# Style steps on ScalarE and GpSimd, one block's z on VectorE, and identity sums in transposing mode

## The reference, cut to what matters

```
# layer 0: adapter, per token
h  = gelu(x @ down_W.T + down_b)                 # 128 -> 32
h  = expert_W[dom] @ h + expert_b[dom] + emb[dom]
x1 = layernorm(h @ up_W.T + up_b + x) * ln_gamma + ln_beta
# layer 1, per block
z  = (x1 - mean) * rsqrt(var + 1e-5)             # per token
h  = z * ln_g + ln_b, normalised over the 256 tokens of the block
se = subj_emb[id];  hyp = relu(se @ hyp_w1 + hyp_b1) @ hyp_w2 + hyp_b2
gamma, beta = split(relu(hyp @ sty_w1 + sty_b1) @ sty_w2 + sty_b2)
gamma = softplus(gamma) + 1e-8
h  = h * gamma + beta                            # style of the block
gates = top 2 of softmax(h @ router_w), renormalised
y  = sum over 8 experts of gate * (relu(h @ w1 + b1) @ w2 + b2)   # 128 -> 512 -> 128
out = x1 + y
```

## Time and profile before

| | |
|---|---|
| median of 3 runs | 119.39 us (118.95 to 119.65) |
| profiled execution, device time | 119.94 us |
| its span in the trace | 118.2 us |
| busy PE / PEld / DVE / ACT / POOL | 112.0 / 84.3 / 91.8 / 84.3 / 54.1 us |
| chain that ended last, largest | PE 72%, DVE 14%, ACT 5%, issue 3%, DMA 3% |
| first expert matmul | at 19.66 us |
| last expert matmul | starts at 112.67 us |
| last output transfer issued | at 115.88 us |

### The profile page before, as it was taken

One profiled execution on the slowest core, in us unless ns is written; L12 is line 12 of the kernel. 1 busy time (PEld: TensorE's weight loads), 2 busy tenths in 40 slices (PEclk: granted clock), 3 DMA queues, 4 the chain that ended last, 5 costly groups with the idle time before them and its releaser, 6 DMA issues.

```text
span 118.2 us, 1665 instructions
## 1 busy us (share of the span) xinstructions
PE 112.0 (95%) x519; PEld 84.3 (71%) x519; DVE 91.8 (78%) x228; ACT 84.3 (71%) x153; POOL 54.1 (46%) x75
## 2 busy tenths in 40 slices
PE   6799988999999999999999999999999999999990
PEld 2157534777777888688888888888888888888780
DVE  4486988999899989997685959595867777776772
ACT  2139845698999988697878787878778687878400
POOL 5020889226417000101259999976758941322310
PEclk9999999999999999999999999999999999999999
DMA  4939699994000000326999300000000000000005
GB/s 68 343 97 365 173 374 442 384 412 150 0 0 3 0 6 0 89 100 165 415 446 408 169 0 6 0 0 0 0 0 0 0 0 0 6 0 0 0 0 178
DMA packets 4473, 14.17 MB, mean 120 GB/s; under 512 B 561, under 2 KB 1905, under 8 KB 4209
## 3 DMA queue, kind: packets, MB, share of 16 engines
q1 hardware_dynamic: 3024, 9.67, 21.9%
q0 software_dynamic: 1008, 3.67, 8.8%
q10 hardware_dynamic: 432, 0.73, 2.2%
HBM read 13.52 MB, written 0.56 MB: 119 GB/s over the span
## 4 chain that ended last, share of the span: by engine, by line
PE 72%; DVE 14%; ACT 5%; issue 3%; DMA 3%; POOL 1%; DVEq 0%; ACTq 0%; POOLq 0%
PE bank L594 22%; PE bank L595 22%; PE bank L633 12%; PE bank L613 11%; DMA ids_i<-ids_dram 3%; DVE x L913 2%; ACT hid_high L508 2%; DVE stats L920 1%; ACT bank L511 1%; DVE hid_low L1005 1%; DVE bank L905 1%; POOL z L370 1%; PE bank L750 1%; DVE stats L876 1%; PE bank L583 1%
## 5 line engine op out<-in xcount | busy, mean ns | idle before, releaser
L508 ACT ACTIVATE hid_high<-bank,early_sb 128x512 fp32r<-128x512 f32 x64 | 44.2, 691 | 15.9 <-PE bank L613 15.8
L1005 DVE TENSOR_TENSOR hid_low<-bank,hid_high 128x512 fp32r<-128x512 f32 x51 | 34.8, 687 | 16.7 <-ACT bank L511 16.1
L511 ACT ACTIVATE bank<-bank,early_sb 128x512 f32<-128x512 f32 x51 | 33.6, 658 | 0.0
L308 POOL TENSOR_TENSOR w_low<-w_raw,w_high 128x256 fp32r<-128x256 f32 x32 | 22.7, 734 | 12.3 <-DMA w_high<-w_all_dram 4.4
L633 PE MATMUL bank<-hid_low,w_high 128*128 128x512 f32 x64 | 25.9, 405 | 0.4 <-DVE hid_low L1010 0.2
L594 PE MATMUL bank<-h_high,w_low 128*128 128x512 f32 x64 | 25.5, 398 | 0.3 <-ACT h_high L486 0.3
L594 PE MATMUL bank<-hid_high,w_low 128*128 128x512 f32 x64 | 25.6, 400 | 0.0
L595 PE MATMUL bank<-h_high,w_high 128*128 128x512 f32 x64 | 25.3, 396 | 0.0
L613 PE MATMUL bank<-h_low,w_high 128*128 128x512 f32 x64 | 25.1, 397 | 0.0
L595 PE MATMUL bank<-hid_high,w_high 128*128 128x512 f32 x64 | 25.0, 390 | 0.0
L318 POOL TENSOR_TENSOR y_sum<-y_sum,y_part 128x512 f32<-128x512 f32 x9 | 11.6, 1292 | 17.3 <-DVE y_part L1025 15.1
(11 more groups left out here) (136 smaller groups left out, 99.2 us busy)
## 6 DMA issues: line engine op xcount, KB each, us to landing
w_high<-w_all_dram POOLq DMA_DIRECT2D x7, 512.0 KB, 7.9
w_raw<-w_all_dram SPq DMA_DIRECT2D x1, 2560.0 KB, 10.9
gate_all<-gate_scratch SPq DMA_DIRECT2D x4, 512.0 KB, 5.9
gate_all<-gate_scratch SPq DMA_DIRECT2D x1, 2048.0 KB, 12.5
w_raw<-w_all_dram SPq DMA_DIRECT2D x3, 512.0 KB, 3.9
style_sb<-style_dram SPq DMA_DIRECT2D x1, 324.0 KB, 5.6
tables_sb<-tables_dram ACTq DMA_DIRECT2D x1, 272.0 KB, 3.8
xT_sb<-xT_dram SPq DMA_DIRECT2D x1, 256.0 KB, 4.4
```

Of the source, the lines that this page charges most:

```text
L308: nc.gpsimd.tensor_tensor(w_low[:, e % W_RING, quarter(q)], w_raw[:, e, quarter(q)], w_high[:, e % W_RING, quarter(q)].bitcast(F32), ALU.s ...
L508: ac(hid_high[:, slot, :], hid_ps[slot][:, :], ACT.Relu, bias=bias).then_inc(relu_steps, 1)
L511: ac(hid_ps[slot][:, :], hid_ps[slot][:, :], ACT.Relu, bias=bias).then_inc(relu_steps, 1)
L1005: v.tensor_tensor(low, ps, high.bitcast(F32), ALU.subtract).then_inc(low_vector, 1)
```

## The change

It does six things. (1) VectorE keeps only the copy of se; hyp1 and hyp2 go to ScalarE, between its other steps, and the rounding of expert 0's weights is spread between them, its last quarter behind softplus' Ln. (2) Softplus' four last steps go to GpSimd, with a second relu of gamma on ScalarE (`gamma_relu`) as one of their inputs. (3) GpSimd does z of tiles 0 and 2 and softplus before the fourth low part of expert 0. (4) z of tile 3 goes from ScalarE to VectorE. (5) VectorE does `centre(1)` and `adapter_out(1)` straight behind those of block 0, and `minus_abs` waits only for gamma_raw. (6) The identity matmuls of `residual` and of the epilogue (L565, L750, L756) are issued with `is_transpose=True`.

```diff
@@ GpSimd
+            def softplus():
+                pool.wait_ge(gamma_relu_ready, 1)
+                pool.wait_ge(soft_ln, 1)
+                nc.gpsimd.tensor_tensor(gamma_T[:, :], gamma_relu[:, :], soft[:, 2, :], ALU.add).then_inc(gamma_steps, 1)
+                pool.wait_ge(gamma_steps, 1)
+                nc.gpsimd.tensor_scalar(gamma_T[:, :], gamma_T[:, :], 1e-8, None, ALU.add).then_inc(gamma_steps, 1)
+                pool.wait_ge(gamma_steps, 2)
+                nc.gpsimd.tensor_scalar(minus_gamma[:, :], gamma_T[:, :], -1.0, None, ALU.mult).then_inc(gamma_steps, 1)
+                nc.gpsimd.tensor_scalar(gamma_g[:, :], gamma_T[:, :], col(C_LNG), None, ALU.mult).then_inc(gamma_steps, 1)
...
             load_high(1)
-            split_lows(0)
+            split_lows(0, (0, 1, 2))
             normalise(0, T)
+            softplus()
+            split_lows(0, (3,))
             split_lows(1, (0, 1))
@@ ScalarE
             token_root(0, tiles(0, 2))
-            round_first_weights((0, 1, 2))
+            act.wait_ge(style_in_psum, 2)
+            ac(hyp1_T[:, :], hyp1_ps, ACT.Relu, bias=col(C_HB1)).then_inc(style_ready, 1)
+            round_first_weights((0,))
+            act.wait_ge(style_in_psum, 3)
+            ac(hyp2_T[:, :], hyp2_ps, ACT.Identity, bias=col(C_HB2)).then_inc(style_ready, 1)
+            round_first_weights((1,))
             act.wait_ge(style_in_psum, 4)
             ac(sty1_T[:, :], sty1_ps, ACT.Relu, bias=col(C_SB1, SC)).then_inc(style_ready, 1)
-            round_first_weights((3,))
+            round_first_weights((2,))
             act.wait_ge(style_in_psum, 6)
             ac(gamma_raw[:, :], gam_ps, ACT.Identity, bias=col(C_SBG)).then_inc(gamma_beta_ready, 1)
+            token_root(1, tiles(0))
+            ac(gamma_relu[:, :], gam_ps, ACT.Relu, bias=col(C_SBG)).then_inc(gamma_relu_ready, 1)
             ac(beta_T[:, :], bet_ps, ACT.Identity, bias=col(C_SBB)).then_inc(gamma_beta_ready, 1)
-            token_root(1, tiles(0))
+            token_root(1, tiles(1))
             soft_exponential()
-            token_root(1, tiles(1))
             soft_logarithm()
-            normalise(T + 1)
+            round_first_weights((3,))
@@ TensorE, residual
                     mm(sum_ps[b][:, t, :], xT_sb[:, (b * T + t) * P:(b * T + t + 1) * P], ident[:, :],
-                       start=(t == 0), stop=False, skip_group_check=True)
+                       is_transpose=True, start=(t == 0), stop=False, skip_group_check=True)
@@ transpose_z
-                    pe.wait_ge(*((z_vector, 1), (z_scalar, 1), None, (z_vector, 2))[b])
+                    pe.wait_ge(z_vector, (1, 2, None, 3)[b])
@@ VectorE, feature_affine
                 after(("f_mean", h))
+                ve.wait_ge(gamma_steps, 4)
                 v.scalar_tensor_tensor(t_gain[:, bs], t_off[:, bs], col(C_LNB), minus_gamma[:, bs], ALU.subtract, ALU.mult
@@ minus_abs
-                ve.wait_ge(gamma_beta_ready, 2)
+                ve.wait_ge(gamma_beta_ready, 1)
@@ VectorE's list
             sum_stats(1)
-            style_step(0)
             token_mv(0, 0, HB)
-            style_step(1)
+            style_step()
             ve.wait_ge(ln0_loaded, 16)
             centre(0)
-            style_step(2)
+            centre(1)
             adapter_out(0)
-            centre(1)
+            adapter_out(1)
             x1_stats(0)
-            adapter_out(1)
             token_mv(1, 0)
             x1_stats(1)
             minus_abs()
...
             normalise(1)
             x1_shift(1)
-            softplus(0)
-            softplus(1)
-            softplus(2)
+            normalise(T + 1)
             feature_stats(0)
```

More of the change, by code:

```diff
@@ L138, in adapter_moe @@
         gamma_raw = sb("gamma_raw", [P, B])
+        gamma_relu = sb("gamma_relu", [P, B])
         beta_T = sb("beta_T", [P, B])
@@ L215, in adapter_moe @@
         gamma_beta_ready = sem("gamma_beta_ready")
+        gamma_relu_ready, gamma_steps = sem("gamma_relu_ready"), sem("gamma_steps")
         soft_in, soft_exp, soft_ln = sem("soft_in"), sem("soft_exp"), sem("soft_ln")
@@ L219, in adapter_moe @@
         z_affine, z_ready, zT_in_psum = sem("z_affine"), sem("z_ready"), sem("zT_in_psum")
-        z_vector, z_scalar = sem("z_vector"), sem("z_scalar")
+        z_vector = sem("z_vector")
         scale_ready, affine_ready, h_ready = sem("scale_ready"), sem("affine_ready"), sem("h_ready")
@@ L474, in soft_logarithm @@
                 ac(soft[:, 2, :], soft[:, 1, :], ACT.Ln, bias=1.0).then_inc(soft_ln, 1)
[L476 to L479, removed]
             def round_h(h):
@@ L756, in _ @@
                     last = mm(sum_last[b - HB][:, t * P:(t + 1) * P], y_part[:, 1, j * P:(j + 1) * P], ident[:, :],
-                              start=False, stop=True, skip_group_check=True)
+                              is_transpose=True, start=False, stop=True, skip_group_check=True)
                 last.then_inc(yT_in_psum, 1)
@@ L821, in _, with style_step @@
                             ).then_inc(up_eff_ready, 1)
[L824 to L829, removed]
-                    v.tensor_scalar(hyp1_T[:, :], hyp1_ps, col(C_HB1), 0.0, ALU.add, ALU.max).then_inc(style_ready, 1)
-                else:
-                    v.tensor_scalar(hyp2_T[:, :], hyp2_ps, col(C_HB2), None, ALU.add).then_inc(style_ready, 1)
+            def style_step():
+                ve.wait_ge(style_in_psum, 1)
+                v.tensor_copy(se_T[:, :], se_ps).then_inc(style_ready, 1)
             def minus_abs():
-                ve.wait_ge(gamma_beta_ready, 2)
+                ve.wait_ge(gamma_beta_ready, 1)
                 v.scalar_tensor_tensor(soft[:, 0, :], gamma_raw[:, :], -1.0, gamma_raw[:, :], ALU.mult, ALU.min
                                        ).then_inc(soft_in, 1)
-            def softplus(k):
-                if k == 0:
-                    ve.wait_ge(soft_ln, 1)
-                    v.scalar_tensor_tensor(gamma_T[:, :], gamma_raw[:, :], 0.0, soft[:, 2, :], ALU.max, ALU.add
-                                           ).then_inc(vec_steps, steps.add())
-                elif k == 1:
-                    after("softplus")
-                    v.tensor_scalar(gamma_T[:, :], gamma_T[:, :], 1e-8, None, ALU.add).then_inc(vec_steps, steps.add())
-                else:
-                    after("softplus")
-                    v.tensor_scalar(gamma_g[:, :], gamma_T[:, :], col(C_LNG), None, ALU.mult
-                                    ).then_inc(vec_steps, steps.add())
-                    v.tensor_scalar(minus_gamma[:, :], gamma_T[:, :], -1.0, None, ALU.mult
-                                    ).then_inc(vec_steps, steps.add())
-                mark["softplus"] = steps.n
             mark = {}
```

## The result

The changed kernel takes **121.39 us** (median of 6 runs, 121.17 to 122.18) against 119.25 of the kernel before (6 runs, 118.94 to 119.74) on the same chip: 1.0188 of it, interval 1.0159 to 1.0217. That is 2.14 us slower, outside the forecast's range of 118.3 to 119.7. Ratios are taken without executions that lie more than 1.5% above the fastest of their kernel, which are three of ten in experiment e3 and one of ten in e11. The profiled execution has a span of 119.6 us. The page shows at once what no row of before had: the granted clock leaves full speed.

What follows compares the result with a forecast made beforehand. TensorE was taken as the bound, its long full stretch only movable as a whole. Prologue 0.23 plus epilogue 0.25 made 0.48 us off the profiled execution, 0.55 off the 119.39 median: 118.9 us, range 118.3 to 119.7.

Steps and rivals of the forecast that it cites:

- the sum's assumption that TensorE's clock holds: Whole kernel: 0.23 us off the prologue plus 0.25 off the epilogue, 0.48 in all, with no clock loss counted.
- The rival: TensorE's prologue: idle time lowers its clock, expert matmuls start at the lower level, 2 us lost, 120.9 us; chance 0.07.
- h_low to get better (0.06): Prologue: VectorE's first h_low subtraction meets no GpSimd subtraction, 0.41 for 0.65 us; h_ready 0.4 earlier, counted as 0.06.
- The style chain: Prologue, hyp1 to second root: gamma_raw starts 0.39 us later, yet block 1's root ends 0.22 earlier.
- The two hops between: Prologue, hyp1 to hyp2 to sty1: each a ScalarE step, matmul pair and two handovers, some 0.70 us.
- the forecast's figure for the prologue: Up to the first expert matmul: 0.17 + 0.06 = 0.23 us off, bounds 0 and 0.4.
- z tiles: Prologue: GpSimd's z of tile 2 takes 0.51 us beside VectorE's tile 3 and ends 0.17 earlier.
- Full exclusion, the rival: Prologue: an exclusive port lock puts z of tile 2 behind tile 3; prologue gain 0, 119.1 to 119.2 us; chance 0.10.
- Softplus on GpSimd: Prologue: four instructions take 0.94 us in all, hidden, 0 on the path; the far bound costs 0.5.
- the sign: Prologue, sign of a right forecast: softplus' four on GpSimd below 0.25 us each and over by 17.5 us.
- GpSimd's delay comes back: Block 2: late expert 2 subtractions hold VectorE's z_shift up to 0.7 us; 0.5 comes back, about 119.4; chance 0.14.
- The epilogue: After the expert work: halved records, adds at 0.33 us, SyncE issues 0.43 apart; 0.25 us off, bounds 0 and 0.45.

Runs made afterwards that it cites:

- e3: Kernel before with only transposing mode added, in the residual sums and the epilogue; 119.79 us over ten runs, ratio 1.0016.
- e11: e9 with hyp1 and hyp2 back on VectorE in the old step order, plain residual sums, no added warm matmuls; 118.98 us, ratio 0.9971.
- e13: e9 without its five added warm matmuls; 122.05 us, ratio 1.0216.
- e1: Changed kernel with five warm matmuls added in TensorE's gaps, behind residual(2) and residual(3); 120.99 us, ratio 1.0125.
- e14: e9 with GpSimd's low parts put back where the change had them; 120.70 us, ratio 1.0113.
- e8: Kernel before with expert 1's last two low parts moved ahead of the issue of expert 2's and 3's high weights; 119.87 us, ratio 1.0066.
- e7: Changed kernel with e1's warm matmuls and GpSimd's remaining low parts waiting for h_ready, behind the high-weight issues; 119.33 us, ratio 1.0015.
- e15: e11 with one warm matmul behind residual(2); 118.90 us, ratio 0.9962.
- e9: e7 with gamma_relu's tile allocated behind all other tiles; 119.07 us, ratio 0.9975.
- e12: e11 with the epilogue's identity sums plain again; 119.05 us, ratio 0.9975.

## Why the prediction was wrong

**The step that failed** is the sum's assumption that TensorE's clock holds; the clock alone cost 2.9 us in e13. The rival had the mechanism: less work and two waits in 9.6 to 13.0 us. It put TensorE's busy time there at 1.9 us (2.43 measured, 2.21 in the stretch that corresponds), its price at 2 us and its time at 120.9. It got 0.07, on the ground that the clock read 1.00 throughout before. That was no evidence: before, the stretch was full, and the change is what empties it. The rival also had the place of the loss wrong. It let the expert matmuls start at the lower level; they start at the full one, and the loss lies ahead of them: the six warm matmuls took 1.27 us more and stood ahead of the transposes of both blocks. Behind them nothing that block 1's chain gained could count.

**The wait it missed** is GpSimd's. The text followed the postponed low parts to the transfers of experts 2 and 3 and to z_shift of block 2, and only expected h_low to get better (0.06). That term failed as well: the next two low parts move along with the postponed ones and meet h_low as before, 0.64 us for the first in after and 0.73 and 0.95 in e1. It did not put 16.9 to 19.0 us of GpSimd beside VectorE's affine steps of the same microseconds, though it had charged minus-abs by just that rule. e14 prices it at 1.65 us, over three times the gain that was forecast; e8 shows it in the kernel before.

**The style chain**. Forecast: gamma_raw 0.39 later, the second root 0.22 earlier all the same. Counted from the first statistics, gamma_raw starts at 3.99 us before and at 4.65 to 4.80 in after, e1 and e7: 0.66 to 0.81 later. Two terms were too short. Hyp1 starts at 2.18 and not at 2.00, as ScalarE does the whole of the first root before it; and from sty1 to gamma_raw it is 1.07 us in e1 in place of 0.95, in after 1.23 at the lower clock. The two hops between take 1.40 us together in e1, as forecast (its own terms make 0.74 for a hop, though, not 0.70). Behind gamma_raw the list runs as forecast, 1.41 us to the root's end in e1 (forecast 1.46).

The root ends at 6.06 before, at 6.21 in after, 6.06 in e1 and e7. The forecast gain is gone with the clock held as well: block 1's transposes start at 6.98 in e1, 6.93 before. With hyp1 and hyp2 on VectorE and the rest moved it is there: 5.79 in e11 (0.27 earlier), and e15's first expert matmul comes 0.23 earlier than before. That this is the forecast's figure for the prologue is luck, since another edit makes it.

**z tiles.** 0.52 us on GpSimd for tile 2 beside VectorE's tile 3, forecast 0.51: right. Full exclusion, the rival, did not happen there, while the 128x2 steps with two inputs were held to the end of GpSimd's subtractions, as it says.

**Softplus on GpSimd.** 0.20, 0.24, 0.23 and 0.29 us; forecast below 0.25 each. The four take 1.12 us in place of 0.94 and are over 7.97 us behind the first statistics in e1 and e7, where 7.65 was forecast and 7.80 was the sign. Somewhat too slow, then, but right in what counts: in e1, e7 and e15 t_gain doesn't wait for it.

**GpSimd's delay comes back** at block 2: it did not. The two z_shifts of block 2 took 0.27 us together, at 29.32 in after. GpSimd's two subtractions of expert 2 ran from 24.68 to 26.10, because its weights came 5.7 us behind their issue and not 8.0; that was the rival's own way out (landing before 26.5).

**The epilogue**. The records are halved as forecast, in the timeline of after:

```profile
113.84 0.50 PE L649 MATMUL bank<-hid_low,w_high 128*128 128x512 f32 x1 [0.17 <-DVE hid_low L1003]
114.62 0.60 PE L766 MATMUL bank<-ident,y_sum 128*128 128x128 f32 x4
...
115.17 1.41 DVE L1154 TENSOR_TENSOR z<-bank,x 128x256 f32<-128x256 f32 x4
115.95 1.48 SPq L295 DMA_DIRECT2D out_dram<-z  x3
```

From the last expert matmul to the last issue it is 3.21 us before, 3.09 in after: 0.12 off instead of 0.25. VectorE's four adds go at 0.33 as forecast; what was mis-sized is SyncE, whose three issues come 0.44 and 0.55 apart, and I took 0.43. The transfer behind them then took 0.34 longer, which no step of the forecast held. Where the tile stands last (e9) the whole is 5.44 against 5.50, and e11 against e12 puts the mode of the epilogue at 0.07 us in the medians, less than they can tell.

## What to carry to other kernels

Before taking work away from TensorE in a prologue, lay its waits and the granted clock side by side: filler that stands ahead of real work costs nearly double once the clock falls (2.74 us against 1.47), and an order of steps that leaves the gaps short (e11, e15) gets by with one filler or none where the other had five (e9). When a queue of GpSimd is postponed, list what VectorE does in the microseconds it moves to, above all tiny steps on the path with two SBUF inputs. And when one loss is mended, look at the profile again before believing in it: here the second was hidden by the first.

## What the runs showed of the hardware beyond that

A 128x2 step of VectorE, 0.16 to 0.29 us alone, takes 0.57 to 0.85 beside GpSimd's 128x256 subtraction (e1, e8), and GpSimd's own subtractions lengthen as well, from 0.72 to 0.77 and 0.94 beside h_low in e1. T_off is a tensor_scalar and was held like those with two inputs; z's 128x128 tensor_scalar was not, and the runs don't say why. Whether the clock falls differs between executions of the same program: e3 kept it in five of ten. Moving one tile of 16 bytes for each partition from the midst of the tiles to their end took 128 KB output transfers from 2.3 to 2.0 us (after and e7 against e9).
